# Own-node attention logits: constant added in the spreads' copy out of PSUM, leaky step and two clears moved from VectorE to GpSimd, transposes started after four pieces

## The reference

```python
e = jax.nn.leaky_relu(el[src_e] + er[dst_e], NEG_SLOPE)      # 4 heads, slope 0.2
m = jax.ops.segment_max(e, dst_e, num_segments=N_NODES)
ex = jnp.exp(e - m[dst_e])
denom = jax.ops.segment_sum(ex, dst_e, num_segments=N_NODES)
alpha = ex / denom[dst_e]
```

## Time and profile before

| | |
|---|---|
| median of 3 runs | 2698.41 us (2687.91 to 2700.14) |
| the profiled execution's own time | 2691.94 us |
| its span in the trace | 2690.2 us |
| DVE busy | 2032.5 us, 76% |
| POOL busy | 1794.9 us, 67% |
| PE busy | 1939.1 us, 72% |

### The profile page before, as it was taken

One profiled execution on the slowest core, in us unless ns is written; L12 is line 12 of the kernel. 1 busy time (PEld: TensorE's weight loads), 2 busy tenths in 40 slices (PEclk: granted clock), 3 DMA queues, 4 the chain that ended last, 5 costly groups with the idle time before them and its releaser, 6 DMA issues. The chain is left out here.

```text
span 2690.2 us, 39714 instructions
## 1 busy us (share of the span) xinstructions
PE 1939.1 (72%) x11638; PEld 1482.3 (55%) x11638; DVE 2032.5 (76%) x3738; ACT 1097.5 (41%) x2303; POOL 1794.9 (67%) x1700
## 2 busy tenths in 40 slices
PE   2564545479899859889849989987989994111397
PEld 2554445458566448756537856656856663100397
DVE  5776676587688577688669968759879887878597
ACT  0433333334344124343214423313336666545398
POOL 6777777556577736477745657773657774777587
PEclk9776666689887569986759967657989997555699
DMA  3444444301265201155413445521334332222386
GB/s 71 126 127 116 115 107 115 99 28 63 65 149 141 53 15 64 59 133 136 96 19 123 157 108 143 124 49 50 108 94 87 85 84 49 66 73 78 131 277 204
DMA packets 350502, 268.21 MB, mean 100 GB/s; under 512 B 177348, under 2 KB 298753, under 8 KB 350268
## 3 DMA queue, kind: packets, MB, share of 16 engines
q1 hardware_dynamic: 302012, 215.05, 26.7%
q0 software_dynamic: 43904, 48.80, 10.5%
q10 hardware_dynamic: 4372, 1.82, 0.3%
HBM read 138.64 MB, written 130.91 MB: 100 GB/s over the span
## 5 line engine op out<-in xcount | busy, mean ns | idle before, releaser
L1153 POOL DMA_INDIRECT edge<-table,row_of_source x588 | 556.3, 946 | 223.1 <-issue 174.6
L943 POOL TENSOR_TENSOR scaled<-edge 128x512 f32<-128x512 f32 x196 | 320.3, 1654 | 320.8 <-PE banks L1078 202.1
L1011 DVE TENSOR_TENSOR_SCAN wide<-keep,wide,banks 64x256 f32<-64x256 uint8 x392 | 292.0, 745 | 94.7 <-issue 54.4
L1051 ACT ACTIVATE scaled_t<-banks 128x1024 f32<-128x1024 f32 x196 | 190.7, 1022 | 274.1 <-PE banks L1078 274.1
L1201 PEld LDWEIGHTS banks<-w_edge_full,wide 128*128 128x128 f32 x1176 | 215.6, 274 | 97.7 <-issue 70.3
L1292 ACT ACTIVATE wide<-h_new 64x512 f32<-64x512 f32 x147 | 92.6, 630 | 429.4 <-DVE h_new L1239 420.9
L1635 POOL DMA_INDIRECT node_rows<-rows_conv,scatter_row x196 | 202.7, 1034 | 86.7 <-issue 55.4
L1194 PE MATMUL banks<-wide,w_row 128*64 128x512 f32 x294 | 236.8, 902 | 30.7 <-DVE h_new L1239 19.8
L1201 PE MATMUL banks<-w_edge_full,wide 128*128 128x72 f32 x1176 | 223.8, 356 | 31.6 <-DVE self_logit L1249 31.6
L208 POOL DMA_INDIRECT edge<-in_x_dram,src_row x196 | 191.4, 977 | 70.9 <-issue 58.8
L1382 POOL DMA_INDIRECT edge<-table,row_of_x x196 | 186.7, 952 | 75.5 <-issue 61.2
(11 more groups left out here) (302 smaller groups left out, 4520.7 us busy)
## 6 DMA issues: line engine op xcount, KB each, us to landing
node_rows<-x_out SPq DMA_DIRECT2D x97, 256.0 KB
wide<-node_rows SPq DMA_DIRECT2D x48, 512.0 KB, 4.6
table<-chain_rows SPq DMA_DIRECT2D x147, 136.0 KB
table<-rows SPq DMA_DIRECT2D x147, 136.0 KB, 2.0
x_again<-x_dst SPq DMA_DIRECT2D x98, 128.0 KB, 2.3
nodes<-in_x_dram SPq DMA_DIRECT2D x97, 128.0 KB, 3.0
table<-x_out SPq DMA_DIRECT2D x97, 128.0 KB
out_dram<-n_soft SPq DMA_DIRECT2D x48, 256.0 KB, 3.0
```

The costliest lines, as they stand in the source:

```text
L943: pool.tensor_tensor(scaled[:, s, SHARE:], edge[:, mine, 0:D].unsqueeze(2).broadcast_to([P, TPG - SHARE, H, D]), inner(edge[:, mine, D:ROW ...
L1011: v.tensor_tensor_scan(out=wide[0:D, bass.ds(first + 1, HALF_E)], data0=keep[:, s, half * HALF_E:(half + 1) * HALF_E], data1=bank[2 + s][h ...
L1051: s_.activation(scaled_t[:, s], banks[:, 6 * s:6 * s + 2], ACT.Copy).then_inc(taken, 1)
L1153: pool.indirect_dma_start(out=edge[:, at_tile], out_offset=None, in_=tables[l], in_offset=bass.IndirectOffsetOnAxis(ap=row_of_source[:, at ...
```

## The change

Three things are moved and one wait is split. The constant of the next layer is added to the own logits in `combine`, where they are copied out of PSUM, so the softmax stage has no addition for them. Their leaky step leaves DVE and is done on POOL by the new function `own_leaky`, in another form: min(x, 0) times (0.2 - 1) into `raised` as scratch (784 columns), and then x plus that in two sums, of 448 and 336 columns. The clears of `chain` go to POOL as well, behind it. PE waits for four leaky pieces of the edges before its first four transposes and for seven before the other three, where it waited for all seven; and likewise for POOL's first and second sum.

```diff
+                PACKS = (slice(0, GE // P), slice(GE // P, CT))
+                by_tile = lambda a: a.rearrange("p (s b h) -> p b s h", b=CT, h=H)
+                def own_leaky(pool):
+                    own_logit = self_logit[:].rearrange("p t h -> p (t h)")
+                    sloped = raised[:, 0:TILES * H]
+                    pool.tensor_scalar(sloped, own_logit, 0.0, SLOPE - 1.0, ALU.min, ALU.mult).then_inc(self_sloped, 1)
+                    pool.wait_ge(self_sloped, 1)
+                    for tiles in PACKS:
+                        pool.tensor_tensor(leaky[:, 1, tiles].rearrange("p b (s h) -> p b s h", h=H), by_tile(own_logit)[:, tiles],
+                                           by_tile(sloped)[:, tiles], ALU.add).then_inc(self_leaky, 1)
+                    for n, start in enumerate((-BIG, 0.0)):
+                        pool.memset(chain[:, n], start).then_inc(chain_set, 1)
...
-                    for n, start in enumerate((-BIG, 0.0)):
-                        link(v.memset(chain[:, n], start))
-                    for n, e in enumerate((edge[:, :, D:ROW], self_logit[:])):
-                        if l > 0:
-                            link(v.tensor_tensor(e, e, const_logit[:, l].unsqueeze(1).broadcast_to([P, TILES, H]), ALU.add))
-                        for b in range(CT):
-                            of = e[:, b:TILES:CT]
-                            v.scalar_tensor_tensor(out=leaky[:, n, b].rearrange("p (s h) -> p s h", h=H), in0=of, scalar=SLOPE,
-                                                   in1=of, op0=ALU.mult, op1=ALU.max).then_inc(leaky_ready, 1)
+                    e = edge[:, :, D:ROW]
+                    if l > 0:
+                        link(v.tensor_tensor(e, e, const_logit[:, l].unsqueeze(1).broadcast_to([P, TILES, H]), ALU.add))
+                    for b in range(CT):
+                        of = e[:, b:TILES:CT]
+                        v.scalar_tensor_tensor(out=leaky[:, 0, b].rearrange("p (s h) -> p s h", h=H), in0=of, scalar=SLOPE,
+                                               in1=of, op0=ALU.mult, op1=ALU.max).then_inc(leaky_ready, 1)
...
+                        v.wait_ge(chain_set, 2)
                         v.tensor_copy(chain[:, n, :, H:H + Q].rearrange("a b (s h) -> a b s h", h=H),
...
-                    for n in range(2):
-                        t.wait_ge(leaky_ready, CT * (n + 1))
+                    for n, (ready, first) in enumerate(((leaky_ready, (GE // P, CT)), (self_leaky, (1, 2)))):
                         for b in range(CT):
+                            if b % 4 == 0:
+                                t.wait_ge(ready, first[b // 4])
...
-                        v.tensor_scalar(self_logit[:, tiles], here[:, :, D + H:], 0.0, None, ALU.add).then_inc(self_ready, 1)
+                        v.tensor_tensor(self_logit[:, tiles], here[:, :, D + H:], const_logit[:, l + 1].unsqueeze(1).broadcast_to([P, TPG, H]),
+                                        ALU.add).then_inc(self_ready, 1)
```

More of the change, by code:

```diff
@@ L713, in softmax_weights @@
                 both = leaky[0:Q].rearrange("p n b q -> p (n b q)")[:, 0:CE]
-                raised = mem(st, f"raised_{l}", [Q, CE])
+                raised = mem(st, f"raised_{l}", [P, CE])
                 denominator = sem(st, f"denominator_{l}")
@@ L721, in softmax_weights @@
                 leaky_ready = sem(st, f"leaky_ready_{l}")
+                self_sloped = sem(st, f"self_sloped_{l}")
+                self_leaky = sem(st, f"self_leaky_{l}")
+                chain_set = sem(st, f"chain_set_{l}")
+                def own_leaky(pool):
[8 more added lines that the diff above has]
+                        pool.memset(chain[:, n], start).then_inc(chain_set, 1)
                 logit_t = sem(st, f"logit_t_{l}")
@@ L748, in _ @@
                     def _(pool):
+                        own_leaky(pool)
                         count = [0]
@@ L771, in _ @@
                             link(pool.tensor_copy(to[:], delta[:]))
+                else:
+                    @block.gpsimd
+                    def _(pool):
+                        own_leaky(pool)
                 @block.sync
@@ L828, in _ @@
                     v.wait_ge(exped, 1)
-                    local(keep_q, ALU.mult, ALU.add, 0.0, raised[:])
+                    local(keep_q, ALU.mult, ALU.add, 0.0, raised[0:Q])
                     v.wait_ge(exped, 2)
-                    link(v.tensor_tensor(both, logit[:, 1], raised[:], ALU.subtract))
+                    link(v.tensor_tensor(both, logit[:, 1], raised[0:Q], ALU.subtract))
                     v.wait_ge(scanned, 4)
@@ L855, in _ @@
                         s_.wait_ge(shifted, n + 1)
-                        s_.activation(raised[:] if n == 0 else logit[:, n], logit[:, n], ACT.Exp).then_inc(exped, 1)
+                        s_.activation(raised[0:Q] if n == 0 else logit[:, n], logit[:, n], ACT.Exp).then_inc(exped, 1)
                     for n, cols in enumerate(parts):
```

## The result

The changed kernel takes 2703.07 us, median of 20 runs, where the kernel before takes 2691.61 us in 20 runs beside them. The ratio is 1.0038, 95% interval 1.0029 to 1.0047. So the change costs about 10 us by the ratio (the two medians lie 11.5 us apart), 0.4%: slower, less than the half per cent that the prediction set as its bound, and three times the 3.4 us that it worked out.

The account below looks back on a forecast made before the run. Bound in each softmax stage start: two chains ending within 0.02 us, one over PE and ACT, one DVE's own. Layers 1 to 3 +2.3 and layer 0 +1.1 make +3.4 us, giving 2698.6 us, range 2688 to 2708.

Parts of the forecast that it names:

- If POOL cost DVE nothing: Softmax stage start: without holds, the scan starts at 4.19 us for 5.41, gaining 1.22 us in layers 1 to 3.
- What POOL costs DVE: Softmax stages: DVE stands still during most of POOL's three steps, held 0.77, 0.61 and 0.60 us, together 1.98 per layer.
- Layers 1 to 3: Softmax starts: all POOL holds fall before the fourth edge piece, scan at 6.17 us, +0.76 per layer, +2.3 in sum.
- the full hold: Main case, softmax stages: POOL and DVE take turns, the holds cost 1.98 us per layer, +3.4 in all; chance 0.55.
- PE should never wait for self_leaky by over 1 us: Sign, softmax stages: POOL's sums are done by about 4.4 us, before PE comes to them at 5.6.
- The slow form: Rival, softmax stages: POOL's sums over strided columns take twice the hold, +8.9 us in sum, 2704.1; chance 0.10.
- the change doesn't reach the end: Rival, softmax stages: the gain and the holds cancel, +1.2 us in sum, 2696.4; chance 0.17.
- Layer 0: Softmax stage of layer 0: +0.4 us at the scan's start and +0.7 from the later numbering, together +1.1.
- The own logits and the clears: Softmax stages: POOL's sums and the clears are done before they are needed, covered by the scans; cost nothing.
- The spreads' copy: Spreads: 147 copies at 161 ns become additions, whose neighbour of that form takes 158; nothing, at most 0.4 us.
- The spreads or messages, where I see no step that changes: Outside the softmax stages: nothing changes there; a move over 13.5 us would have to come from them.
- Theory B: Rival in the follow-up runs' forecasts: the other 8 us, as in layer 2's messages and the last stretch, are caused too.

Follow-up runs that it names:

- e3: Changed kernel with the own logits' leaky pieces back on DVE behind those of the edges, clears still on POOL; ratio to the kernel before 0.9985, on a slower chip.
- e7: The same kernel as e3, run again: own logits' leaky pieces on DVE, the rest as changed; ratio to the kernel before 1.0002, on a slower chip.
- e12: Changed kernel with own leaky pieces and clears on DVE, no POOL code for them in layers 1 to 3; 2692.16 us, ratio to the kernel before 0.9999.
- e11: Changed kernel with POOL waiting for all seven edge pieces before its first step; 2707.85 us, ratio to the kernel before 1.0062.
- e2: Changed kernel, unedited, run again for a second trace on a slower chip; ratio to the kernel before 1.0004.
- e6: Changed kernel, unedited, run once more on a slower chip; ratio to the kernel before 1.0018.
- e10: Changed kernel with the two clears of chain back on DVE, behind the edge pieces; 2700.03 us, ratio to the kernel before 1.0025.
- e9: As e3, but POOL clears three single columns in place of its one-input step and two sums; 2689.06 us, ratio to the kernel before 0.9986.
- e5: Kernel before the change, unedited, run once more on a slower chip; ratio 1.0008.
- the last four experiments: e9, e10, e11 and e12, run on a chip like the first; the kernel before took 2693.42 us beside e9.

## Why the prediction was right, and by how much it was off

*The side and the range* held: slightly slower, inside 0.5% of no change. The size was three times the forecast, and that the total fell into the range was in part luck. The forecast was 2.3 us in layers 1 to 3, 1.1 in layer 0, nothing elsewhere; between the two spans there are 0.1, 2.3 and 8.4. The step from median to median, 11.5 us, is more than the +8.9 that the range allowed for; 2703.07 lies inside because the range let the base go up to 2698.4, and 20 runs put it at 2691.61.

*"If POOL cost DVE nothing"*, 1.22 us per stage: right. e3, e7 and e12 give 1.20.

*"What POOL costs DVE", 1.98 us per stage*: mis-sized, 1.17 measured in layer 3 (0.52 at the first scan's start, 0.65 in the backward scan). The reason is in the step under "Layers 1 to 3": that all of POOL's steps come beside the addition and the first four pieces. POOL's one-input step takes 2.83 us with little beside it (e11) and 3.66 beside DVE, not the 1 us that the step took for granted, and it holds DVE once, for about 0.5 us. In layer 0 of the changed kernel, where there is no addition, it takes 2.89 us beside the seven pieces: the other 0.8 come with the addition. Its first sum then falls where DVE waits for ACT and holds nobody; its second waits behind the forward scan and holds the backward one. So each of layers 1 to 3 changed by 0.0 us and not by +0.76. The exclusion that the Trainium skill states for a GpSimd instruction and a VectorE one with two SBUF inputs ("SBUF — State Buffer", section "SBUF: two separate sides") is seen again here in the 2.65 and 2.89 us of the backward scan. The one-input step doesn't follow it throughout: six of DVE's seven pieces run beside it at 0.26 us each, and in e11 the scan runs beside its last 1.1 us in 2.02. Here the measurement decides; why that step differs isn't shown.

*The signs and the rivals.* First scan at 4.71 us and not 6.2, excesses of 0.5 us on DVE ahead of it and not 2: the full hold as worked out fell. "PE should never wait for self_leaky by over 1 us" fell too: PE waits 1.47 us for POOL's second sum, which is itself behind the forward scan. The slow form fell: the first sum takes 1.13 us for 448 columns, where twice the hold would be 1.54; the second takes 2.61, but only 0.69 of it lie behind the end of the scan. Nearest in the softmax stages came "the change doesn't reach the end": it had +1.2 us there, and they show 2.4, or 0.9 without the low clock of layer 0, of which below.

*Layer 0*, +1.1 forecast: +2.3 in the first trace, +0.3 and +0.8 in e2 and e6. In the first trace 1.5 us of it are TensorE's clock. Windows of the stage's end, before and after, with PEclk in the column behind the busy times:

```profile
567.20:569.90 2.70, 1.80 (x15) 1.55 (x16) 0.51 (x1) 0.96 (x3) 0.25 (x1) 1.00 0.00 0
```

```profile
567.50:571.70 4.20, 3.28 (x15) 2.88 (x15) 0.51 (x1) 1.01 (x3) 0.23 (x1) 0.61 0.00 0
```

Seven transposes and eight idle products (`keep_warm`) ran at full granted clock before, 0.92 and 1.04 us, and mostly at the lower of the two levels after, 1.57 and 1.92. PE had done the same products ahead of them in both, and then waited 0.56 us before and 1.08 after. e10 shows the same low clock. e2, e6 and e11 waited as long or longer (1.34, 1.09, 1.26 us) and had the full clock, so the wait alone doesn't explain it, and why the clock stayed low stays open. At full clock the stage is 0.3 us (e2) to 0.8 us (e6) longer than before, under the 1.1.

*The own logits and the clears*, cost nothing: right, but barely for the logits. POOL was done 7.4 us after the stage's start (1828.27), not 4.4, and ACT had the own logits at 1829.80 (the second copy of that timeline, 1829.31 + 0.49), 0.44 us ahead of the join at 1830.24; e11 shows what comes past that. The clears e10 bears out.

*The spreads' copy*, at most 0.4 us: near enough. The instruction takes 161 to 163 ns in the mean for 161. In e9 and e12, which carry it on a chip like the first, the three spreads take 744.2 and 743.8 us together for 743.3.

*"The spreads or messages, where I see no step that changes"*: this step failed, for these stages do change. The gathers of the last spread and of the stretch behind take 952 to 955 and 955 to 958 ns in all five traces with POOL's leaky steps and 944 to 947 in the nine without; on the faster chips that is the 1.5 and 2.1 us. That it comes with these steps is shown; by what it comes about is open. Their number is excluded by e9; their kind, their encoding and what they leave behind in the engine aren't told apart.

*Layer 2's messages*, 4.0 us of the 10.8, stay open. Theory B said that the change brings on the slow turns; e10, which has POOL's steps and 145.45 us, and e12, which has none and 152.10, speak against it. So does e5, in which the kernel before goes over to turns of 5.88 by itself. Six traces of two kernels fall apart three against three by chance one time in ten, and that isn't excluded. The traces show that the turns of 5.88 us keep going once begun; what starts them isn't shown. By the two traces a changed kernel with the quick turns would be 6 us faster in this stage. So of the 10.8 us between the spans about 6 are tied to the change by a place in the trace: 2.3 in layer 0, of which 1.5 by the low clock, and 3.6 in the gathers. 4.0 are those turns, and about 1.4 of the stretch behind have no cause here. That the tie is to POOL's steps is what the comparison with e12 shows, with 9.8 us and the slow turns in both.

## What to carry to other kernels

Before moving work off an engine, ask whether a shorter wait elsewhere has already made it free: here splitting PE's wait and dropping the addition left DVE idle for longer than its seven own pieces take, and keeping them there takes 4.4 us off the softmax stages (e9; ratio 0.9986, part of it by layer 2's messages). Where DVE's instruction has two SBUF inputs and POOL's is a two-input sum, count on the two taking turns: what is saved on DVE can come back as a hold on the DVE instruction that happens to come next, here a scan (2.65 us for 2.00). A one-input step of POOL was milder, one hold of about 0.5 us in 3.66. And a difference of 0.1 to 0.3% between two kernels can lie wholly in a stage that neither edit touched, as e9 and e12 have it (layer 2's messages, 144.8 and 152.1 us), so compare the traces stage by stage before giving it a cause.

## What the runs showed that was not expected

A gather instruction of POOL behind layer 3 took 944 to 947 ns in nine traces and 955 to 958 in five, with the same statement, tile and table; what goes with it is the POOL work of earlier stages. Two engines that take turns have several rhythms, 5.51, 5.70 or 5.88 us per turn, and the slowest, once begun, was kept to the end of the stage, over 100 us in five traces. And chips differ: the same program took 2692 us in the runs of the result, 2693 on the chip of the last four experiments, and 3243 and 3248 on two others, with spreads of about 330 us for 248, while the softmax stages agreed to 0.05 us in layers 1 to 3.
